# The routing stage of a token router: rank steps from the last tile to the first, one finish for all tiles, and a square-root table loaded ahead

## The reference, cut to what matters

```python
def _L0_ffn_ref(hidden_states, w_router, W1, b1, W2, b2):
    B, S, D = hidden_states.shape
    k = int(S * CAPACITY_FACTOR)              # 0.5: 1024 of 2048
    scores = jnp.einsum('bsd,d->bs', hidden_states, w_router)
    top_scores, top_idx = jax.lax.top_k(scores, k)
    weights = jax.nn.sigmoid(top_scores)
    selected = jnp.take_along_axis(hidden_states, top_idx[:, :, None], axis=1)
    h = jax.nn.gelu(jnp.einsum('bkd,df->bkf', selected, W1) + b1)
    processed = jnp.einsum('bkf,fd->bkd', h, W2) + b2
    update = weights[:, :, None] * processed
    def scatter_one(xb, ib, ub):
        return xb.at[ib].add(ub)
    output = jax.vmap(scatter_one)(hidden_states, top_idx, update)
    return output

x = x + _L0_attn_a_ref(_layernorm(x), ...)
x = x + _L0_ffn_ref(_layernorm(x), ...)
x = x + _L0_attn_b_ref(_layernorm(x), ...)
x = x + _L0_ffn_ref(_layernorm(x), ...)
```

## Time and profile before

| what | us |
|---|---|
| median of 3 runs | 1870.37 |
| the runs | 1862.95, 1870.37, 2165.05 |
| profiled execution, its own time | 1865.69 |
| its span, slowest core (core 4) | 1864.1 |
| spans of the 8 cores | 1854.3 to 1864.1 |
| PE busy | 1652.6 (89% of the span) |
| DVE busy | 903.2 (48%) |
| ACT busy | 698.3 (37%) |
| POOL busy | 191.4 (10%) |

### The profile page before, as it was taken

One profiled execution on the slowest core, in us unless ns is written; L12 is line 12 of the kernel. 1 busy time (PEld: TensorE's weight loads), 2 busy tenths in 40 slices (PEclk: granted clock), 3 DMA queues, 4 the chain that ended last, 5 costly groups with the idle time before them and its releaser, 6 DMA issues.

```text
span 1864.1 us, 23704 instructions; the slowest of 8 cores (1854.3 to 1864.1 us)
## 1 busy us (share of the span) xinstructions
PE 1652.6 (89%) x8182; PEld 792.1 (42%) x8330; DVE 903.2 (48%) x1738; ACT 698.3 (37%) x1059; POOL 191.4 (10%) x243
## 2 busy tenths in 40 slices
PE   1999999933999996999999999999999997399997
PEld 1444444412444443545544444444444443244443
DVE  4899997897112227166434333542224445621122
ACT  4899998348232114402333221431111112624210
POOL 2222222110100013000000000000010000100002
PEclk9999999975899997999999999999999998599999
DMA  9877676564577759900101010774276001374466
GB/s 277 249 249 234 229 259 159 93 102 130 100 109 106 108 132 228 210 1 1 46 1 46 1 46 1 136 117 76 46 120 106 1 1 48 105 225 66 71 91 91
DMA packets 70644, 205.76 MB, mean 110 GB/s; under 512 B 4288, under 2 KB 4352, under 8 KB 70528
## 3 DMA queue, kind: packets, MB, share of 16 engines
q0 software_dynamic: 39424, 93.86, 31.4%
q1 hardware_dynamic: 31104, 110.38, 18.0%
HBM read 229.12 MB, written 33.82 MB: 141 GB/s over the span
## 4 chain that ended last, share of the span: by engine, by line
PE 67%; ACT 10%; DVE 6%; DMA 5%; issue 4%; ACTq 3%; DVEq 2%; SPq 1%; POOL 0%; POOLq 0%
PE v_h1ps L1102 12%; PE v_h2ps L1116 11%; PE mlp_a L1795 6%; PE mlp_a L1807 6%; PE ab_bank L1638 6%; ACT scr_s L463 4%; ACT scr_s L458 3%; PE ab_big L1564 3%; PE ab_bank L1583 3%; PE ab_bank L1590 3%; PE ab_bank L1533 3%; PE mlp_a L1822 3%; PE mlp_r L1822 3%; PE ab_bank L1676 2%; PE ab_bank L1651 2%
## 5 line engine op out<-in xcount | busy, mean ns | idle before, releaser
L1102 PE MATMUL v_h1ps<-m_sel_fm,m_w 128*128 128x512 bf16 x998 | 225.8, 384 | 3.9 <-DVE m_sel_fm L997 1.3
L547 PE MATMUL yps<-ring,diag 128*128 128x512 f32 x448 | 203.0, 606 | 26.8 <-POOL diag L423 26.8
L1116 PE MATMUL v_h2ps<-m_w,m_h1q 128*128 128x512 bf16 x1008 | 221.5, 379 | 0.8
L1015 DVE SCALAR_TENSOR_TENSOR m_acc<-v_h2ps,w_sel,m_acc 128x512 f32<-128x512 f32 x96 | 72.0, 751 | 257.6 <-PE v_h2ps L1116 200.0
L1040 ACT ACTIVATE m_h1q<-v_h1ps,fb_s 128x512 bf16<-128x512 f32 x128 | 88.0, 688 | 282.3 <-PE v_h1ps L1102 282.2
L1102 PEld LDWEIGHTS v_h1ps<-m_sel_fm,m_w 128*128 128x128 bf16 x1024 | 100.8, 99 | 124.3 <-issue 8.4
L631 DVE SCALAR_TENSOR_TENSOR scr_v<-ring,wvs_bc 128x1024 bf16<-128x1024 f32 x128 | 153.3, 1216 | 0.5 <-issue 0.5
L1116 PEld LDWEIGHTS v_h2ps<-m_w,m_h1q 128*128 128x128 bf16 x1024 | 100.2, 98 | 120.8
L1779 ACT ACTIVATE gate_prod<-mlp_a 128x512 bf16<-128x512 f32 x64 | 38.2, 597 | 265.7 <-PE mlp_a L1795 265.5
L547 PEld LDWEIGHTS yps<-ring,diag 128*128 128x128 f32 x448 | 84.0, 193 | 123.7 <-issue 123.6
L1749 DVE TENSOR_TENSOR gate_prod<-mlp_a,gate_prod 128x512 bf16<-128x512 f32 x64 | 44.3, 692 | 143.4 <-PE mlp_a L1807 143.1
(11 more groups left out here) (280 smaller groups left out, 2258.2 us busy)
## 6 DMA issues: line engine op xcount, KB each, us to landing
ring<-x_all SPq DMA_DIRECT2D x64, 1024.0 KB, 9.2
m_w<-fW POOLq DMA_DIRECT2D x16, 2048.0 KB, 17.7
sel_dram<-m_xn SPq DMA_DIRECT2D x32, 264.0 KB, 2.6
y_dram<-x_tok SPq DMA_DIRECT2D x4, 2048.0 KB, 21.3
x_tok<-y_dram SPq DMA_DIRECT2D x16, 512.0 KB, 6.7
x_tok<-y_dram POOLq DMA_DIRECT2D x16, 512.0 KB, 5.4
out<-x_tok SPq DMA_DIRECT2D x4, 2048.0 KB, 15.5
x_tok<-x_all POOLq DMA_DIRECT2D x14, 512.0 KB, 6.6
```

Source lines behind the costliest of these rows:

```text
L547: ii = t.matmul(yps[tt % 2][:, h * 512:(h + 1) * 512], lhsT=diag_of(n), rhs=x_tile(n)[:, h * 512:(h + 1) * 512], start=(n % B == 0), stop= ...
L1102: ii = t.matmul(h1ps[n % 4][:, :], lhsT=w1[:, dt * D + ft * P:dt * D + (ft + 1) * P], rhs=sel_fm[:, dt * D + h * 512:dt * D + (h + 1) * 51 ...
L1116: ii = t.matmul(h2ps[m % 4][:, :], lhsT=h1q[:, ff * D + rt * P:ff * D + (rt + 1) * P], rhs=w2[:, ff * D + h * 512:ff * D + (h + 1) * 512], ...
```

## The change

Signals: `flag` and `pos` count 1 instead of 4. The diagonals, the broadcasts, the rank steps and their sums run from the last group or tile to the first; a step waits only for the broadcast groups that it reads, and for the sums of the step two before it in the new order. `rk` is zeroed ahead of the diagonals, since the finish now reads all 16 x 16 columns of it at once. There is one finish, for all 16 tiles. ScalarE begins the block with a square root of a constant.

```diff
@@ mod_vector
             v.drain()
-            for g in range(4):
+            v.memset(rk[:, 0:256], 0.0)
+            for g in (3, 2, 1, 0):
                 v.tensor_tensor(out=sdg[:, g * 512:(g + 1) * 512].rearrange('p (q t) -> p q t', q=4),
...
             def rank_step(J):
-                v.wait_ge(sem(V + 'bc'), at(V + 'bc', 4))
-                if J >= 2:
-                    v.wait_ge(sem(V + 'rks'), at(V + 'rks', J - 1))
+                v.wait_ge(sem(V + 'bc'), at(V + 'bc', 4 - J // 4))
+                if J < NT - 2:
+                    v.wait_ge(sem(V + 'rks'), at(V + 'rks', NT - 2 - J))
...
-            def rank_finish(g):
-                v.wait_ge(sem(V + 'rks'), at(V + 'rks', 4 * g + 4))
-                lo, hi = 4 * g, 4 * g + 4
-                cols = slice(lo, hi)
-                v.tensor_tensor(out=m_nb[:, cols], in0=m_a1[:, cols], in1=m_a2[:, cols], op=ALU.add)
-                for J in range(lo, hi):
-                    v.tensor_reduce(out=m_red[:, J:J + 1], in_=rk[:, J:J + 16 * J + 1:16], axis=AX, op=ALU.add)
+            def rank_finish():
                 v.drain()
-                v.tensor_tensor(out=m_nb[:, cols], in0=m_nb[:, cols], in1=cS['nlater'][:, cols], op=ALU.subtract)
+                v.tensor_tensor(out=m_nb[:, :], in0=m_a1[:, :], in1=m_a2[:, :], op=ALU.add)
                 v.drain()
-                v.scalar_tensor_tensor(out=m_flag[:, cols], in0=m_red[:, cols], scalar=-(T // 2), in1=m_nb[:, cols], op0=ALU.add, op1=ALU.is_lt)
+                v.tensor_tensor(out=m_nb[:, :], in0=m_nb[:, :], in1=cS['nlater'][:, :], op=ALU.subtract)
+                v.wait_ge(sem(V + 'rks'), at(V + 'rks', NT))
+                v.tensor_reduce(out=m_red[:, :], in_=rk[:, 0:256].rearrange('p (j i) -> p i j', j=NT), axis=AX, op=ALU.add)
                 v.drain()
-                n = min(hi + 1, NT) - lo - 1
-                v.tensor_tensor_scan(out=m_cum[:, lo + 1:lo + 1 + n], data0=cS['ones32'][:, 0:n], data1=m_flag[:, lo:lo + n],
-                                     initial=m_cum[:, lo:lo + 1], op0=ALU.mult, op1=ALU.add).then_inc(sem(V + 'flag'), 1)
-                v.scalar_tensor_tensor(out=m_nb[:, cols], in0=m_flag[:, cols], scalar=0.0, in1=cS['tokbig'][:, cols], op0=ALU.is_equal, op1=ALU.mult)
+                v.scalar_tensor_tensor(out=m_flag[:, :], in0=m_red[:, :], scalar=-(T // 2), in1=m_nb[:, :], op0=ALU.add, op1=ALU.is_lt)
+                v.drain()
+                v.tensor_tensor_scan(out=m_cum[:, 1:NT], data0=cS['ones32'][:, 0:NT - 1], data1=m_flag[:, 0:NT - 1],
+                                     initial=0.0, op0=ALU.mult, op1=ALU.add).then_inc(sem(V + 'flag'), 1)
+                v.scalar_tensor_tensor(out=m_nb[:, :], in0=m_flag[:, :], scalar=0.0, in1=cS['tokbig'][:, :], op0=ALU.is_equal, op1=ALU.mult)
...
-            for J in range(NT):
+            for J in range(NT - 1, -1, -1):
                 rank_step(J)
-                if J >= 4 and J % 4 == 0:
-                    rank_finish(J // 4 - 1)
-            rank_finish(3)
+            rank_finish()
             token_rows()
@@ mod_scalar
+            s.activation(out=st['rstd1'][:, 0:1], in_=cS['eps_ln'][:, :], func=AF.Sqrt)
             s.wait_ge(sem(V + 'inv'), at(V + 'inv', 1))
@@ mod_tensor
-            for g in range(4):
-                t.wait_ge(sem(V + 'sdiag'), at(V + 'sdiag', g + 1))
+            for g in (3, 2, 1, 0):
+                t.wait_ge(sem(V + 'sdiag'), at(V + 'sdiag', 4 - g))
                 t.matmul(bc[:, g * 512:(g + 1) * 512], lhsT=cS['ones32'][:, :], rhs=sdg[:, g * 512:(g + 1) * 512],
                          start=True, stop=True).then_inc(sem(V + 'bc'), 1)
-            def positions(g):
-                t.wait_ge(sem(V + 'flag'), at(V + 'flag', g + 1))
...
-            for J in range(NT):
+            for J in range(NT - 1, -1, -1):
                 c0 = J % 2 * T
-                t.wait_ge(sem(V + 'cmp'), at(V + 'cmp', J + 1))
-                if J >= 4 and J % 4 == 0:
-                    positions(J // 4 - 1)
+                t.wait_ge(sem(V + 'cmp'), at(V + 'cmp', NT - J))
                 for I in range(J, NT):
...
-            positions(3)
+            t.wait_ge(sem(V + 'flag'), at(V + 'flag', 1))
+            t.matmul(pos[:, 0:NT], lhsT=cS['mask_jlt'][:, :], rhs=m_flag[:, :], start=True, stop=False)
+            t.matmul(pos[:, 0:NT], lhsT=cS['ones32'][:, :], rhs=m_cum[:, :], start=False, stop=True).then_inc(sem(V + 'pos'), 1)
```

More of the change, by code:

```diff
@@ L148 @@
     [('v0_rows', 1), ('v1_rows', 1)],
-    [('v0_flag', 4), ('v1_flag', 4)],
-    [('v0_pos', 4), ('v1_pos', 4)],
+    [('v0_flag', 1), ('v1_flag', 1)],
+    [('v0_pos', 1), ('v1_pos', 1)],
     [('v0_gidx', 1)],
@@ L959, in token_rows @@
+                v.scalar_tensor_tensor(out=m_nb[:, :], in0=m_flag[:, :], scalar=0.0, in1=cS['tokbig'][:, :], op0=ALU.is_equal, op1=ALU.mult)
             def token_rows():
                 perm = cS['perm']
-                v.wait_ge(sem(V + 'pos'), at(V + 'pos', 4))
+                v.wait_ge(sem(V + 'pos'), at(V + 'pos', 1))
                 v.drain()
@@ L1053, in mod_tensor @@
                 t.wait_ge(sem('ab_m_xadd'), at('ab_m_xadd', total('ab_m_xadd')))
-            for g in range(4):
-                t.wait_ge(sem(V + 'sdiag'), at(V + 'sdiag', g + 1))
+            for g in (3, 2, 1, 0):
+                t.wait_ge(sem(V + 'sdiag'), at(V + 'sdiag', 4 - g))
                 t.matmul(bc[:, g * 512:(g + 1) * 512], lhsT=cS['ones32'][:, :], rhs=sdg[:, g * 512:(g + 1) * 512],
                          start=True, stop=True).then_inc(sem(V + 'bc'), 1)
-            def positions(g):
-                t.wait_ge(sem(V + 'flag'), at(V + 'flag', g + 1))
-                t.matmul(pos[:, 4 * g:4 * g + 4], lhsT=cS['mask_jlt'][:, :], rhs=m_flag[:, 4 * g:4 * g + 4], start=True, stop=False)
-                t.matmul(pos[:, 4 * g:4 * g + 4], lhsT=cS['ones32'][:, :], rhs=m_cum[:, 4 * g:4 * g + 4],
-                         start=False, stop=True).then_inc(sem(V + 'pos'), 1)
-            for J in range(NT):
+            for J in range(NT - 1, -1, -1):
                 c0 = J % 2 * T
-                t.wait_ge(sem(V + 'cmp'), at(V + 'cmp', J + 1))
-                if J >= 4 and J % 4 == 0:
-                    positions(J // 4 - 1)
+                t.wait_ge(sem(V + 'cmp'), at(V + 'cmp', NT - J))
                 for I in range(J, NT):
```

## The result

The changed kernel takes 0.9943 of the time before, 95% interval 0.9926 to 0.9961. On the 1865.69 us of the profiled execution before that is 1855.1 us (1851.9 to 1858.4); the profiled execution of the changed kernel took 1854.92 us. Of its four executions (1853.47, 1854.92, 1926.22 and 2066.63 us) the last two are disturbed ones, in which the cores of one half of the chip ran at a lower granted clock (0.84 to 0.92 in place of 0.96), and the ratio leaves such executions out. The forecast was 1855 us, within 1846 to 1864. The change is smaller than 2%, as forecast, and its interval leaves out 1.

What follows compares the result with a forecast made beforehand. Bound by one string from root to matmuls, mostly VectorE's: 5.81 us off the first routing (start 0.87, steps 0.87+1.10 region excluded; steps 14 and 15 1.10, finishes 3.66, last finish 0.18), 5.62 off the second; 1855 us, range 1846 to 1864.

Steps and rivals of the forecast that it cites:

- The table: ScalarE, before the root: a dummy root loads the table early, gaining 1.29 us in each routing.
- The memset: VectorE, ahead of the diagonals: zeroing 256 float32 PSUM columns costs 0.28 us.
- The start of the broadcasts: TensorE's four products: shifted 1.01 us earlier, running from 420.69 to 426.84.
- The new wait: VectorE, step 13: waits for step 15's sums, queued behind all four products on TensorE, and starts at 427.10.
- The rank steps: VectorE, step 13 to step 0: same instructions in another order, 21.65 us plus 0.08 us for the accumulator read.
- The finish: VectorE, after step 0: one finish, its reduction 0.42 us, flag at 450.16, first use of the positions at 451.57.
- What is late next: Gather: also waits for ScalarE's normed tiles, but with slack of some 10 us, so the gain passes.
- What the reversal is worth: VectorE's rank steps: taking steps 14 and 15 out of the string in the new order gains 1.10 us.
- (a): Rival, VectorE at step 13: no rest, full overlap with the broadcasts, 1846.7 us; 4 in 100.
- (b): Rival, ScalarE: the table is not loaded ahead, 2.6 us less gain, 1856.9 us; 7 in 100.
- (c): Rival, behind the gather: gain partly given back, say half, 1860 us; 7 in 100.
- (d): Rival, large matmuls: slower through TensorE's lower clock, 1911 us if the whole first round ran low; 2 in 100.

Runs made afterwards that it cites:

- experiment 1: Kernel before plus one line, the square root of a constant ahead of ScalarE's wait, in both routings; ratio to before 0.9979.
- experiment 2: Changed kernel without the square root of a constant; ratio to the kernel before 0.9959.
- experiment 7: Changed kernel with the memset of the sums moved ahead of VectorE's wait for the root; one run, 1859.18 us.
- experiment 5: Changed kernel with own buffer places for the comparisons of steps 15 to 9, which no longer wait for earlier sums; one run, 1852.25 us.
- experiment 6: Changed kernel with TensorE's queue reordered, sums of steps 15 and 14 behind the second broadcast product, 13 and 12 behind the third; one run, 1851.22 us.
- experiment 3: Changed kernel without the square root and with groups, tiles and waits in the old order, leaving one finish and its memset; ratio to before 0.9960.
- the two repeats: The changed kernel as it is, measured again in two later jobs against the kernel before; ratios 0.9954 and 0.9940.
- experiment 8: Changed kernel with own places for the comparisons of steps 15 to 9 and the early memset together; ratio to before 0.9902.
- experiment 9: The changed kernel as it is, five rounds on one chip; ratio to before 0.9940, median 1855.20 us.

## Why the prediction was right, point by point

- **The table.** 1.29 us forecast in each routing; 1.29 alone and 1.28 on top measured (experiments 1 and 2).
- **The memset.** 0.28 us forecast, its row takes 0.27; moving it away shortens the string by 0.25 (experiment 7).
- **The start of the broadcasts.** 2.01 us after the reciprocal by the sum (420.69 - 418.68), 1.99 us measured on all cores.
- **The new wait.** The step that decided the forecast: that the third step waits for `rks` behind all four products, so that the rest for the broadcasts is not gained. A rest of 3.8 us was forecast, 3.01 and 3.04 us seen on core 0, whose broadcasts took 5.56 and 5.96 us against the 6.15 of the sum; over all cores and both routings it is 2.25 to 4.04 us, longer where the broadcasts are. Experiments 5 and 6 show the cause. What I gave for the sums and signals, 0.25 us between the last product and step 13, was 0.52 us in the first routing of core 0 (425.29 to 425.81) and 0.14 us in the second. One size in it was wrong without touching the string: the first product was put at 6.15 / 4 = 1.54 us, but on core 0 only 0.50 of the clock was granted from 419 to 423, while the end of the 6.15 us had 0.83 (426 to 428). So step 15 starts 2.16 us behind the start of the broadcasts (421.89 - 419.73), after a rest of 0.49 us, where the sum had it 1.66 us behind and no rest. Step 13 waits for the sums in any case, so only the rest before it got shorter.
- **The rank steps.** 21.73 us from step 13 to the end of step 0 forecast (21.65 and the accumulator read), 21.69 measured (425.81 to 447.50).
- **The finish.** From the end of step 0 to the reduction 0.83 us forecast, 0.81 measured; the reduction 0.42 and 0.42, so the stride of 16 columns shows no cost here; flag to first use of the positions 1.41 forecast, 1.35 measured.
- **What is late next.** The gap from gather to large matmuls stayed 10.4 us, no transfer came in the way.
- **What the reversal is worth.** The prediction took 1.10 us for steps 14 and 15 out of the string as the gain of the new order. 0.20 us of that is the rest before step 14, which experiment 3 loses too, in the old order, with the finishes gone. The steps themselves bring 0.83 us: from step 0 to the end of step 15 it takes 22.52 us in experiment 3, from step 13 to the end of step 0 21.69 us in the changed kernel. The 16 sums behind the last step take 0.37 us of it back (0.82 us from its end to the reduction, against 0.45), which the prediction counted in the finish, at 0.41. That leaves 0.44 us in the second routing and 0.07 us in the first, where the gap stands, or 0.25 us on the mean; I expected 0.6 us when I wrote down experiment 3. The sum was right because all these terms stood in it, if not each under the edit that brings it.
- **What is luck.** The mechanism was right and the string fell by the 11.4 us forecast. That the time, 1855.1 us, came within a tenth of 1855 is luck: its interval is 3.3 us either way, and the two repeats gave 8.6 and 11.2 us below before (0.9954 and 0.9940).

The rivals: (a), the full overlap, would have shown no rest at the third step; the rest was there, and experiment 5 makes (a) true by another edit and gets 29.5 us of string, near the 29.0 that (a) stands for (32.8 less 3.8). (b) falls with the ScalarE row. (c) and (d) fall with what stands behind the gather: the time from gather to matmul is unchanged, and so is the time from the first large matmul to the last one of the block (225.0 and 225.1 us), which a longer stay at the lower clock level would have stretched.

## What to carry to other kernels

A wait that names less is not yet a shorter wait: after loosening a condition, look at the next condition of the same instruction, and at what stands in front of its signal in the other engine's queue. Here the loosened broadcast wait gave way to a buffer whose release was queued behind the same broadcasts, and 28 of 32 blocks of that buffer were free in the new order. And small finishing steps between large ones on the bounding engine cost their full length (1.22 us, three times, in each routing); doing them once was worth more here (some 4.0 us) than the new order (0.25 to 0.44 us).

## What the runs showed of the hardware that I had not expected

- A gap of some 0.35 to 0.43 us shows up in most of these kernels at one point of one of the two routings, on the cores alike, and its place moves with the code: before L952 in the first routing of the kernel before (0.38 us at the same place in experiment 1), before the third step in the first routing of the changed one, before the flag in the second routing of experiment 5, where VectorE's row on core 7 reads

```profile
1595.17 0.18 DVE L955 SCALAR_TENSOR_TENSOR m_flag<-a_coef 128x16 bf16<-128x16 f32 x1 [0.43 <-issue]
```

In experiment 3 it is in neither, to 0.01 us, and there the string less broadcasts is the same on all cores and in both routings, with a standard deviation under 0.01 us; in the kernel before it is 0.16 and in the changed one 0.19 us, which is the gap. "issue" says only that the profile shows no other cause; I have not tested one.

- The broadcasts take from 5.05 to 6.65 us before and 5.06 to 6.73 us after for identical work. In the trace of before they begin at a granted clock of 0.50 of the full one, and 0.83 was granted in the stretch 426 to 428. Where in them the level rises differs from core to core: in the first routing of the changed kernel core 6 (5.06 us, from 418.75) was granted 0.72 in 421 to 422 and 1.00 in 422 to 424, core 4 (6.59 us, from 422.83) still 0.50 in 425 to 427. This and the gap are nearly the whole scatter of the string.
- The time from gather to large matmul is mostly 9.8 to 11 us, but 14.1 and 13.5 us on cores 2 and 3 in the first routing of experiment 5, 13.5 and 13.4 us on cores 0 and 1 in the second of experiment 1, 13.4 us once in experiment 8, 13.2 us once in experiment 9 and 12.5 us once before. On core 2 of experiment 5 VectorE rests 3.54 us before its last copy of the transposed rows (L997, at 465.70), so the delay arises ahead of that copy. Its cause is open.
